# Three banks in turn for both norms, and a later addition to x, in the feed-forward phases of a four-layer model

## The reference

```python
def _layernorm(x, axis=-1, eps=1e-05):
    m = jnp.mean(x, axis=axis, keepdims=True)
    v = jnp.var(x, axis=axis, keepdims=True)
    return (x - m) / jnp.sqrt(v + eps)
...
        def _qlinear(x, W, b):
            y = q_acc(jnp.einsum('bsk,nk->bsn', q_mul(x), q_mul(W)))
            return q_acc(y + q_mul(b))
```

## Time and profile before

| | |
|---|---|
| three runs | 3308.96, 3311.95, 3316.39 us |
| median | 3311.95 us |
| the profiled execution | 3312.04 us, span 3310.4 us |
| its mean granted clock of TensorE | 0.969 of full speed |
| busy over the span | PE 2831.6 us (86%), DVE 2666.6 (81%), ACT 2258.8 (68%), POOL 1860.7 (56%) |
| instructions | 65685 |

### The profile page before, as it was taken

The page is one execution under the profiler, slowest core; times in us unless marked ns, Lnnn a source line. Parts: engine busy times, 40 slices in busy tenths (PEclk is TensorE's granted clock), DMA queues, the critical chain, the costliest instruction groups (busy, mean ns, idle before and its releaser), DMA issues. The chain is left out here.

```text
span 3310.4 us, 65685 instructions
## 1 busy us (share of the span) xinstructions
PE 2831.6 (86%) x20846; PEld 1477.4 (45%) x20846; DVE 2666.6 (81%) x4380; ACT 2258.8 (68%) x4205; POOL 1860.7 (56%) x1466
## 2 busy tenths in 40 slices
PE   8999989686999999999997678789999779688876
PEld 5666654233444444444442224344444334477732
DVE  6888879536999999999999958769999968444468
ACT  5666658576999898989895427666777558444455
POOL 2333323155889898989897635447777745100046
PEclk9999999898999999999999999989999989899999
DMA  2000001256474747474746232201101012301023
GB/s 88 0 0 0 0 14 45 81 172 175 120 209 135 221 140 222 140 217 141 217 124 185 59 79 74 76 21 25 24 23 25 18 56 89 126 22 23 22 71 78
DMA packets 201533, 294.28 MB, mean 89 GB/s; under 512 B 62242, under 2 KB 179158, under 8 KB 201110
## 3 DMA queue, kind: packets, MB, share of 16 engines
q1 hardware_dynamic: 198678, 288.03, 30.3%
q10 hardware_dynamic: 2688, 4.29, 0.4%
HBM read 190.11 MB, written 102.09 MB: 88 GB/s over the span
## 5 line engine op out<-in xcount | busy, mean ns | idle before, releaser
L1780 POOL TENSOR_TENSOR mam_hc<-mam_h,mam_cs 128x896 f32<-128x896 f32 x336 | 703.5, 2094 | 173.5 <-DVE mam_h L1699 98.7
L1699 DVE TENSOR_TENSOR_SCAN mam_h<-mam_a,mam_kept,mam_dbx 128x448 f32<-128x448 f32 x672 | 737.7, 1127 | 48.4 <-ACT mam_a L1569 47.4
L1422 PE MATMUL mam_ps_y<-mam_hc,mam_ident 128*128 128x448 f32 x1344 | 570.8, 558 | 124.8 <-POOL mam_hc L1780 124.7
L1569 ACT ACTIVATE mam_a<-mam_ft,mam_a_neg 128x448 f32<-128x448 f32 x672 | 409.5, 657 | 77.1 <-DVE mam_h L1699 76.0
L1422 PEld LDWEIGHTS mam_ps_y<-mam_hc,mam_ident 128*128 128x128 f32 x1344 | 249.8, 193 | 425.4 <-POOL mam_hc L1780 216.2
L1686 DVE TENSOR_TENSOR mam_dbx<-mam_ps_u,mam_bs 128x448 f32<-128x448 f32 x672 | 380.7, 610 | 0.0
L682 POOL TENSOR_TENSOR att_prob<-att_prob,att_share 128x588 f32<-128x588 f32 x128 | 149.0, 1186 | 306.8 <-DVE att_share L974 306.8
L2209 POOL TENSOR_TENSOR scan_ch<-scan_h,scan_cs 128x392 f32<-128x392 f32 x192 | 263.7, 1387 | 56.5 <-DVE scan_h L2150 55.3
L368 POOL MEMSET f_squares_ln<- 128x392 f32 x4 | 1.7, 424 | 362.5 <-POOLq L2283 326.5
L387 POOL CAST f_h<-f_hr 128x392 fp8e5<-128x392 f16 x128 | 65.3, 510 | 234.1 <-DVE f_hr L308 234.1
L2150 DVE TENSOR_TENSOR_SCAN scan_h<-scan_decay_by_column,scan_h,scan_drive_by_column 128x392 f32<-128x392 f32 x112 | 196.8, 1757 | 0.0
(11 more groups left out here) (240 smaller groups left out, 6631.1 us busy)
## 6 DMA issues: line engine op xcount, KB each, us to landing
mam_taps<-normed SPq DMA_DIRECT2D x220, 130.5 KB
mam_bs<-dram_bc SPq DMA_DIRECT2D x56, 448.0 KB, 9.1
mam_cs<-dram_bc SPq DMA_DIRECT2D x56, 448.0 KB, 11.7
normed<-f_staged SPq DMA_DIRECT2D x96, 203.0 KB
mam_ft<-dram_steps SPq DMA_DIRECT2D x42, 448.0 KB, 4.8
f_mixed<-mixed SPq DMA_DIRECT2D x64, 196.0 KB, 2.4
mam_gt<-dram_gs SPq DMA_DIRECT2D x48, 224.0 KB, 2.7
dram_gs<-mam_gs SPq DMA_DIRECT2D x47, 224.0 KB, 2.8
```

The lines of the kernel that those rows point to most:

```text
L1422: mm = pe.matmul(ps_y[p % 2][:, 0:MT], ident[:], hc[t % 2][:, i, :], start=False, stop=(t % 8 == 7 and i == 1))
L1569: act.activation(a[t % 3][:, i, :], ft[p % 2][:, 0, :], ACT.Exp, scale=a_neg[:, at:at + 1]).then_inc(decays, 1)
L1699: dve.tensor_tensor_scan(h[:, n % 8, :], a[t % 3][:, i, :], dbx[:, i, 0:MT], kept[:, at:at + 1], ALU.mult, ALU.add).then_inc(scanned, 1)
L1780: pool.tensor_tensor(hc[t % 2][:], h[:, row:row + 2, :], cs[:, 2 * pair:2 * pair + 2, :], ALU.mult).then_inc(weighed, 1)
```

## The change

Four things are done in all four feed-forward phases. The centred chunks of both norms lie in one ring of three PSUM banks: chunk c's first centring in bank 2c mod 3, its second in bank (2c+1) mod 3, and the waits of the two centrings follow from that. GpSimd's `update(c)` waits, besides for the bias, until VectorE has cast the inner units of chunk c+1. GpSimd's loop is written with other indices. The loops of VectorE, ScalarE and TensorE are written out, slot by slot, and the last layer has one slot less.

```diff
-        fronts = [buf.psum(f"xc_ff{p}", [P, BANK]) for p in range(2)]
-        xc_ln = buf.psum("xc_ln", [P, BANK])
+        ring = [buf.psum(f"centred{p}", [P, BANK]) for p in range(3)]
...
-            for s in range(3):
-                slot(s, 0, s, active(s))
-            with eng.Fori(0, CHUNKS // UNROLL - 1) as t:
-                for i in range(3, 3 + UNROLL):
-                    slot(t * UNROLL + i, t + i // UNROLL, i % UNROLL, [True] * 4)
-            for s in range(CHUNKS - 1, CHUNKS + 3):
-                slot(s, s // UNROLL, s % UNROLL, active(s))
...
+        end = CHUNKS + (2 if last else lag)
+
+        def bank(c):
+            return ring[2 * c % 3]
+
+        def second_bank(c):
+            return ring[(2 * c + 1) % 3]
+
+        def is_chunk(c):
+            return 0 <= c < CHUNKS
...
                 def update(c):
 
                     pool.wait_ge(ff["biased"], c + 1 + fb)
+                    pool.wait_ge(ff["hidden8"], min(c + 2, CHUNKS) + fb)
                     pool.tensor_tensor(x[:, c * N:(c + 1) * N], x[:, c * N:(c + 1) * N],
                                        yb[:], ALU.add).then_inc(ff["updated"], 1)
...
-                quantize_third(0)
-                for c in range(CHUNKS):
-                    if c + 1 < CHUNKS:
-                        quantize_third(c + 1)
-                    update(c)
+                for c in range(CHUNKS + 1):
+                    if is_chunk(c):
+                        quantize_third(c)
+                    if is_chunk(c - 1):
+                        update(c - 1)
                     if c + AHEAD_ADDED < CHUNKS and not in_place:
                         add_mixed(c + AHEAD_ADDED)
...
-                def subtract_mean(s, name, base, ready, reader, c, u):
-
-                    if ready == "updated":
-                        pe.wait_ge(ff["updated"], c + 1 + fb)
-                    elif not in_place:
-                        pe.wait_ge(ff["added"], c + 1 + ab)
-                    held = int(name == "ff")
-                    if base > 0 or not isinstance(c, int) or c > held:
-                        pe.wait_ge(s[reader], c + base - held)
-                    to = fronts[u % 2] if name == "ff" else xc_ln
-                    pe.matmul(to[:, 0:N], centre[:], x[:, bass.ds(c * N, N)],
-                              start=True, stop=True).then_inc(s["centred"], 1)
+                def centre_of(s, to, c):
+                    pe.matmul(to[:, 0:N], centre[:], x[:, c * N:(c + 1) * N],
+                              start=True, stop=True).then_inc(s["centred"], 1)
+
+                def subtract_mean(c):
+
+                    if not in_place:
+                        pe.wait_ge(ff["added"], c + 1 + ab)
+                    reached(pe, ff["quantized"], c - 2 + fb)
+                    if not last:
+                        reached(pe, ln["normed"], c - 4 + nb)
+                    centre_of(ff, bank(c), c)
+
+                def subtract_mean_again(c):
+
+                    pe.wait_ge(ff["updated"], c + 1 + fb)
+                    pe.wait_ge(ff["quantized"], min(c + 3, CHUNKS) + fb)
+                    reached(pe, ln["normed"], c - 2 + nb)
+                    centre_of(ln, second_bank(c), c)
```

More of the change, by code:

```diff
@@ L331, in add_bias, with norm @@
                                       ALU.add).then_inc(ff["biased"], 1)
-                def norm(c, turn, u):
+                def norm(c):
                     dve.wait_ge(ln["scaled"], c + 1 + nb)
[L337 to L341, removed]
+                    reached(dve, st.stored[c % 2], (c // 2 + layer * (CHUNKS // 2)) * 16)
+                    dve.tensor_tensor(staged[c % 2][:, :, 1:SIDE + 1],
+                                      second_bank(c)[:, 0:N].rearrange("c (r q) -> c r q", q=SIDE),
                                       rstd["ln"][:].rearrange("c (r q) -> c r q", q=SIDE),
                                       ALU.mult).then_inc(ln["normed"], 1)
-                def slot(s, turn, u, on):
-                    if on[1]:
+                for s in range(end):
+                    if is_chunk(s - 1):
                         round_third(s - 1)
-                    if on[0]:
-                        quantize(s, u)
-                    if on[1]:
+                    if is_chunk(s):
+                        quantize(s)
+                    if is_chunk(s - 1):
                         rectify_third(s - 1)
-                    if on[2]:
+                    if is_chunk(s - 2):
                         round_result(s - 2)
-                    if on[1]:
+                    if is_chunk(s - 1):
                         rectify(s - 1, 0)
-                    if on[2]:
+                    if is_chunk(s - 2):
                         add_bias(s - 2)
-                    if on[1]:
+                    if is_chunk(s - 1):
                         rectify(s - 1, 1)
-                        quantize_hidden(s - 1, (u - 1) % 2)
-                    if not last and on[3]:
-                        norm(s - lag, turn - int(u < lag), (u - lag) % UNROLL)
-                slots(dve, slot)
+                        quantize_hidden(s - 1)
+                    if not last and is_chunk(s - lag):
+                        norm(s - lag)
             @block.gpsimd
@@ L403, in _, with square @@
                 act.wait_ge(st.prepared, prep0 + preps - 9)
-                def square(s, name, base, c, u):
+                def square(s, name, base, c):
                     act.wait_ge(s["centred"], c + 1 + base)
-                    from_ = fronts[u % 2] if name == "ff" else xc_ln
+                    from_ = bank(c) if name == "ff" else second_bank(c)
                     act.activation(squares[name][:], from_[:, 0:N], ACT.Square
@@ L426, in round_hidden @@
                                    ).then_inc(ff["hidden16"], 1)
-                def slot(s, turn, u, on):
-                    if on[0]:
+                square(ff, "ff", fb, 0)
+                for s in range(end):
+                    if is_chunk(s):
                         inverse_deviation(ff, "ff", fb, eps_t, "quantized", s)
-                    if on[1]:
+                    if is_chunk(s - 1):
                         round_hidden(s - 1)
-                    if not last and on[3]:
-                        square(ln, "ln", nb, s - 3, u)
-                    if has_next(s):
-                        square(ff, "ff", fb, s + 1, u + 1)
-                    if not last and on[3]:
+                    if not last and is_chunk(s - lag):
+                        square(ln, "ln", nb, s - lag)
+                    if is_chunk(s + 1):
+                        square(ff, "ff", fb, s + 1)
+                    if not last and is_chunk(s - lag):
                         inverse_deviation(ln, "ln", nb, eps_c, "normed", s - lag)
-                square(ff, "ff", fb, 0, 0)
-                slots(act, slot)
             @block.tensor
```

56 lines of the change are left out of this document (24 added, 32 removed).

## The result

| | before | after |
|---|---|---|
| median of 20 runs each | 3311.52 us | 3319.05 us |
| all runs | 3304.39 to 3318.87 | 3309.85 to 3325.84 |
| profiled execution, span | 3312.04, 3310.4 | 3321.65, 3320.1 |

The ratio is 1.002, with a 95% interval of 1.0012 to 1.0028: slower by 7.5 us, about as much as can be told from no change. 3332 was forecast, slower by 20.5. A second series of the same kernel gave 3317.74 and 1.0019 (1.0006 to 1.0032).

A forecast was written before the change was run, and what follows sets the result against it. No engine is full; cycles of waits set the slot. Layer 0 -1.4 - 3, layer 1 +14.2 - 3, layer 2 +13.9 - 3 and layer 3 +2 sum to +19.7 us: 3332 us, range 3317 to 3348.

The forecast's parts named there:

- loops written out: TensorE, VectorE and ScalarE lose register arithmetic and branches but fetch more code; value taken nothing, at worst 5 us.
- three banks: Second centring no longer waits for the last norm: layer 0 -1.4 us in its slots, phase ends -3 in layers 0 to 2.
- new order of the additions: GpSimd's earlier additions still wait for loads behind norm(c): 5.17 us a slot, +14.2 and +13.9 us in layers 1 and 2.
- 4.54 us cycle through `ps_y`: Layers 0 to 2: the bank holding second norm's variance and second product in turn limits the slot to 4.54 us at best.
- The other cycle: Layers 0 to 2: through the single bank `xc_ln`, norm, centring, square, variance, log, exp, 4.50 us; three banks cut it.
- the +2: Layer 3: its two-slot cycle goes from 3.93 to 4.01 us a slot, +2 us, with bounds -5 and +8.
- The 2.58 us of the load: Layers 1 and 2: time from load's issue to addition, taken as constant; 0.2 more or less moves both by 5 us together.
- Absorbed: Rival: delay taken only every other slot, or phase ends give more; 7 us less in layers 1 and 2, 3318 or below; chance 0.10.
- Earlier additions cost nothing: Rival: loads ready a slot early, layers 1 and 2 gain 4.4 us each, layer 3 gains 5; 3294 us; chance 0.05.
- Blocked VectorE: Rival: GpSimd's later updates and additions block VectorE's fast operations, above all in layer 3; +18 us, 3350 us; chance 0.12.
- The clock: Rival: TensorE falls to 1.2 GHz as its busy share drops in layers 1 and 2; +47 us, 3379 us; chance 0.03.
- the likeliest case: The forecast itself, 3332 us in all, chance 0.70, own range from load landing, layer 3 and code, 3320 to 3345.

The follow-up runs named there:

- five-ahead kernels: The kernel before (3533.99 us) and the changed kernel (3747.53 us), each with loads of the mixer's output issued five chunks ahead in place of six; one run each.

## Why the prediction was wrong by 13 us, and what of it held

Of the 13 us, 8.4 lie in the feed-forward phases (+11.3 for +19.7). The experiments split the change into its parts. Each line is the difference of two kernels' feed-forward phases, in us:

| part | forecast | measured | from |
|---|---|---|---|
| loops written out | 0 | -9.2 | 644.1 (loops alone) - 653.3 (before, mean) |
| three banks | -1.4 - 3 x 3 = -10.4 | -8.6 | 635.5 (banks and loops) - 644.1 |
| new order of the additions | } +14.2 + 13.9 + 2 | +27.4 | 662.9 (all but the wait) - 635.5 |
| the new wait | } = +30.1 | +1.6 | 664.5 (after, mean) - 662.9 |
| sum | +19.7 | +11.3 | |

The split depends a little on the order in which the parts are taken. With the new order first it costs 25.9 us (679.2 - 653.3), and loops and banks then give 16.3 (679.2 - 662.9) and not 17.8. Loops and banks together are off from their 10.4 by 7.4 us in the first order and 5.9 in the second, the larger part of the 8.4 both times. No run has three banks with the loops kept, so what the banks would give by themselves in the slots isn't known; after the loops they give nothing there (4.51 us with and without them), and their gain is at the ends of phases.

**The step that failed** is "The loops written out [...] Value taken: nothing". They gave 9.2 us in the phases and 0.27% in the runs, more than the measured difference of the whole change. The prediction counted 0.05 us a slot in layer 0, down to the 4.54 us cycle through `ps_y`, and left nothing for the loops. But that cycle was read in one of the short slots: the norms of before stood 4.53, 4.62, 4.53 and 4.69 us apart in turn, and in the kernel with the loops alone it is 4.51 in every slot. The other cycle was read without its last handover. "4.50 us, and the norm starts there" isn't so: the exp ends at 550.63 and the norm starts at 550.75, so that cycle took 4.62, the length of its slot. A cycle read from a trace is no floor when the change touches the engines' programs.

What the loops' code cost can be read in the trace of before, which holds the register and branch instructions too, though the rows here leave them out. Between exp and norm VectorE has one register operation of 0.05 us (at 550.66 for the norm of 550.75) wherever the handover is 0.65 or more, in every second slot, and none where it is 0.56. TensorE's sequencer has one of 0.05 us at 546.84, between the wait for the norm and the weights' load for the centring at 546.94, in every slot of the loop; with the loops written out there is none at either place. The first centring behind the loop, whose slot the kernel before has written out too, comes 0.71 us behind its norm there as well. So work on registers (addresses and semaphore values) makes the two handovers longer. The loop's branch comes once in four slots, on VectorE at 555.38, and that slot is the one of 4.69 us, 0.07 longer than the other long one of 4.62; in layer 1 it is 4.79 for 4.64. The branch's slot thus has a fifth to a third of the 0.3 to 0.5 us by which four slots were longer than 4 x 4.51, and the rest comes without a branch. No run took out one without the other.

The Trainium skill, page Advanced Engine Details and Errata, section "Control Flow Timing", gives some 51 ns for a branch and 108 for one with a comparison, which spread over four slots would be an estimated 27 ns a slot at most on one engine. The 9.2 us over 28 x 3 slots are 110 ns a slot, so the trace agrees that more than a branch was saved.

By layer the phases missed the forecast by -0.7, -2.1, -2.4 and -3.3 us. The loops alone gave -1.9, -3.7, -4.0 and +0.4. So the miss of layer 3 isn't theirs: there the +2 was mis-sized, as shown below.

**Layers 1 and 2.** The mechanism held step by step: load behind norm(c), addition, cast, update, norm(c+2), with the DMA named in front of 26 additions. Its length was 10.09 and not 10.33 us: the load landed in 2.46 us (2.58 taken), addition and cast took 1.42 (1.60), update to centring 0.98 (1.08), while centring to norm took 3.90 (3.7). In 26 slots that is 2.6 us a layer. Measured over both profiles, the first 28 norms took 12.2 and 13.1 us more than before (+14.2 and +13.9 forecast), the last four 2.5 and 4.1 us less where -3 stood, and the starts of the phases 0.7 and 0.5 less. With the loops of before still in place the pairs were 10.25 us on average ((2114.29 - 1991.28) / 12 in the trace with the new order alone). Together +9.1 and +8.6 for +11.2 and +10.9. The 2.58 us of the load, taken as a constant, is none: in these two layers most loads land 2.3 to 3.0 us behind their issue, but one to three in a phase take 3.3 to 4.1, in both kernels. In layer 2 of the changed kernel two took 3.81 and 3.62, and the pairs of slots behind them 11.4 and 12.6 us, not 10.1.

**Layer 3.** +2 was forecast, -1.3 measured. The timeline of the kernel after:

```profile
3220.96 0.93 POOL L369 TENSOR_TENSOR all_x<-all_x,f_yb 128x392 f32<-128x392 f32 x1 [0.57 <-DVE f_h L310]
...
3222.79 1.02 POOL L362 TENSOR_TENSOR all_x<-all_x,f_mixed 128x392 f32<-128x392 f32 x1 [0.91 <-DMA f_mixed<-mixed]
3222.86 1.07 DVE L293 TENSOR_SCALAR f_hr<-f_h,f_b 128x392 f16<-128x392 f16 x1
...
3223.97 0.75 DVE L310 CAST f_h<-f_hr 128x784 fp8e5<-128x784 f16 x1
...
3224.20 0.37 SPq L211 DMA_DIRECT2D f_mixed<-mixed  x1
...
3226.72 1.01 POOL L362 TENSOR_TENSOR all_x<-all_x,f_mixed 128x392 f32<-128x392 f32 x1 [0.93 <-DMA f_mixed<-mixed]
...
3228.79 0.93 POOL L369 TENSOR_TENSOR all_x<-all_x,f_yb 128x392 f32<-128x392 f32 x1 [0.57 <-DVE f_h L310]
```

The cycle is the one forecast: update, stores and load 3.24 us (3220.96 to 3224.20), landing 2.52, addition to update 2.07, with VectorE's rectification and cast held up by GpSimd. It comes to 7.83 us over two slots, for 8.02. Over 27 slots the phase is still 0.4 us longer than before (106.5 for 106.1 us between updates), its start 1.0 longer, and its end, for which the prediction had no term in this layer, 2.7 shorter: -1.3. The parts went far apart before they cancelled: the wait alone costs this layer 8 us (153.0 against 145.0), and the early addition takes them back.

**Layer 0.** The slot is 4.51 us, for 4.54, and -5.1 us came for -4.4. The wait's price of nothing in layers 0 to 2 held with the old order: 28 norms take 121.8 or 121.9 us in each of the three layers, with it and without. (The phases of layer 0 differ by 3.0 us, all of it ahead of the first norm.) With the new order the phases of layers 1 and 2 are 3.2 and 1.5 us longer with it, too near the spread of the profiles to call a price. The wait also does what was said of the casts, 562 ns, and that this is worth nothing where VectorE waits anyway is shown by 3282.04 with it and 3282.05 without.

**The rivals.** *Absorbed* had 3318 or below, by a delay taken only in part. The time came out next to it, but not the cause: the norms' pairs are 10.1 us apart, near the forecast. *Earlier additions cost nothing* is out by the experiment with the new order alone. *Blocked VectorE* is seen in layer 3 (1.07 and 0.75 us), as an accounted part of the cycle and not on top of it. *The clock* stayed between 0.98 and 1.00 in the windows of the phases of the changed kernel, in both profiles, and the five-ahead kernels show that it was a real way for such a cycle to go.

**The numbers.** 3319.05 lies in the range given, near its lower end, and under the likeliest case's own range of 3320 to 3345. Slower by over 0.2% had 0.87; the interval, 0.12% to 0.28%, has that bound in its middle. The time is inside by the range's width: of the 20.5 us forecast a little over a third came. "Norms 5.2 us apart" was 5.06 to 5.13 over the first 26 slots. The sign "if layer 0 falls under 4.5" for a wrong reading of the cycle through `ps_y` did not appear (4.51), though 4.54 was no floor.

**What stays open.** The phases lost 11.3 us, the runs' medians 7.5, and all the rest was 3 us shorter in the profiles of the changed kernel, though its code is the same. Over the profiles of this study that rest lies between 2645 and 2659 us with no order that follows an edit. Whether the missing 4 us are this spread or an effect on what follows a phase was not told apart.

## What to carry to other kernels

Count, for each load that waits for a result, how many slots lie between that result and the first one that needs what was loaded: the loop's length over that number is a floor for the slot. Here one loop of about 10 us gave 5.1 us a slot where it spanned two slots and 11.4 where it spanned one, at a lower clock; where it spanned four it did not bind, and other waits set 4.51. A loop that binds also lets late loads through, as the pairs of 11.4 and 12.6 us show. An edit that moves a consumer earlier has to move the issue of its load too: the same change with loads eight ahead takes 3282 us, under both kernels. And before a cycle read from a trace is used as a floor, ask whether the change also takes instructions out of its handovers.

## What the hardware showed that was not expected

Written-out loops made two handovers between engines 0.1 us shorter (0.81 to 0.71 us in every slot, 0.65 to 0.56 in every second).

VectorE's rectification, from 16-bit to 16-bit numbers, took 0.31 us and beside GpSimd's addition 1.07 (it ended at 3223.93, the addition at 3223.81); the cast behind it took 0.75 for 0.56, beside GpSimd's cast. In both kernels they are held up for about as long as GpSimd's instruction still runs. By this the trace agrees with the rule of the exclusive lock that the prediction cites from the Trainium skill's page SBUF — State Buffer.

TensorE's granted clock, 0.98 to 1.00 in every feed-forward window of the changed kernel, was 0.83, 0.76 and 0.53 over the stretches shown of the two kernels with loads five ahead. In the first of them TensorE sat idle for 2.62 us in the slot shown, and centring and variance then took 1.67 and 1.51 us for 0.92 and 0.90. So a wait that grew twofold cost more than its own length.
